# Seven block products for half the hidden channels of the expert layer's second product, and edge counts summed two tiles ahead of their mask

## What is computed

```python
_ACTS = [_gelu, jax.nn.silu, _mish, _gelu]
pooled = x.mean(axis=1)
logits = pooled @ router_w.T + router_b
top_v, top_i = jax.lax.top_k(logits, TOP_K)
...
h = jnp.einsum('bld,edh->belh', x, w1) + b1[None, :, None, :]
h = jnp.stack([_ACTS[i](h[:, i]) for i in range(e)], axis=1)
out = jnp.einsum('belh,ehd->beld', h, w2) + b2[None, :, None, :]
y = jnp.einsum('be,beld->bld', gate, out) + x
```

## Time and profile before

| | us |
|---|---|
| median of 3 runs | 2633.81 |
| lowest and highest | 2632.14, 2635.10 |
| profiled execution, its time | 2630.19 |
| profiled execution, its span | 2628.4 |

### The profile page before, as it was taken

The page is one execution under the profiler, slowest core; times in us unless marked ns, Lnnn a source line. Parts: engine busy times, 40 slices in busy tenths (PEclk is TensorE's granted clock), DMA queues, the critical chain, the costliest instruction groups (busy, mean ns, idle before and its releaser), DMA issues.

```text
span 2628.4 us, 26650 instructions
## 1 busy us (share of the span) xinstructions
PE 2555.2 (97%) x10594; PEld 1813.6 (69%) x10594; DVE 1587.2 (60%) x2708; ACT 769.6 (29%) x1291; POOL 347.7 (13%) x197
## 2 busy tenths in 40 slices
PE   7999999999999997999999999999999999999999
PEld 4667667558965996777777775565755786556676
DVE  4456471779948996987888998254342561341322
ACT  1043342006732863222222221430002331332000
POOL 0888888000000000000000000000000000000000
PEclk9999999999999998999999999999999999999999
DMA  9232313543020406000120003200450100213201
GB/s 257 26 44 14 50 2 50 143 145 123 20 80 20 116 1 215 1 0 1 72 102 0 24 24 115 70 1 1 115 164 18 37 1 1 63 37 126 87 24 59
DMA packets 139168, 160.74 MB, mean 61 GB/s; under 512 B 96618, under 2 KB 108484, under 8 KB 137516
## 3 DMA queue, kind: packets, MB, share of 16 engines
q1 hardware_dynamic: 68323, 158.60, 19.4%
q0 software_dynamic: 70720, 0.43, 2.8%
HBM read 122.75 MB, written 35.87 MB: 60 GB/s over the span
## 4 chain that ended last, share of the span: by engine, by line
PE 51%; DVE 7%; ACT 2%; issue 1%; DMA 0%; SPq 0%; DVEq 0%; ACTq 0%
PE psum L521 51%; DVE arena L1863 2%; DVE arena L1865 1%; DVE arena L1864 1%; PE psum L532 0%; DVE arena L1856 0%; ACT arena L1126 0%; ACT arena L1131 0%; ACT arena L1015 0%; DVE arena L1519 0%; DVE arena L1929 0%; DVE arena L1361 0%; DVE arena L1862 0%; DVE arena L1855 0%; DVE arena L1888 0%
## 5 line engine op out<-in xcount | busy, mean ns | idle before, releaser
L521 PE MATMUL psum<-arena 128*125 128x384 f32 (+12 forms) x9762 | 2454.4, 413 | 34.8 <-DMA arena<-in_ffn_w 7.1
L521 PEld LDWEIGHTS psum<-arena 128*125 128x125 f32 (+3 forms) x9762 | 1719.8, 188 | 745.5 <-issue 136.7
L2278 POOL DMA_INDIRECT count_matrix<-arena x170 | 343.0, 2018 | 121.1 <-DVE arena L1458 59.7
L1863 DVE RECIPROCAL arena<-arena 128x500 f32<-128x500 f32 x60 | 196.7, 3278 | 2.1
L1613 DVE CUSTOM_DVE_ANT_0 arena<-arena 125x1250 bf16<-125x1250 bf16 (+1 forms) x100 | 139.2, 1458 | 12.9 <-DMA arena<-source_rows 8.3
L2288 POOL MEMSET arena<- 125x60 f32 x1 | 0.2, 208 | 1039.4 <-PE psum L521 1039.4
L1697 DVE TENSOR_TENSOR arena<-arena 125x1250 f32<-125x1250 f32 x80 | 116.3, 1453 | 13.7 <-ACT arena L1108 13.6
L1105 ACT ACTIVATE arena<-arena 125x1250 f32<-125x1250 f32 x80 | 106.9, 1336 | 56.7 <-PE psum L521 56.5
L1700 DVE SCALAR_TENSOR_TENSOR arena<-arena 125x1250 f32<-125x1250 f32 x80 | 116.9, 1461 | 2.8
L1015 ACT ACTIVATE arena<-psum 128x250 f32<-128x250 f32 (+1 forms) x102 | 40.6, 494 | 231.4 <-PE psum L532 230.9
L1248 ACT ACTIVATE arena<-psum,arena 128x250 f32<-128x250 f32 x120 | 49.3, 465 | 198.6 <-PE psum L521 198.6
(11 more groups left out here) (226 smaller groups left out, 1435.0 us busy)
## 6 DMA issues: line engine op xcount, KB each, us to landing
arena<-in_ffn_w SPq DMA_DIRECT2D x3, 4608.0 KB, 14.9
residual<-arena SPq DMA_DIRECT2D x30, 336.0 KB
arena<-residual SPq DMA_DIRECT2D x30, 336.0 KB
arena<-target_rows SPq DMA_DIRECT2D x12, 610.4 KB
arena<-in_gat_w SPq DMA_DIRECT2D x3, 2304.0 KB, 10.5
arena<-residual SPq DMA_DIRECT2D x10, 672.0 KB
residual<-arena SPq DMA_DIRECT2D x10, 672.0 KB
count_matrix<-arena SPq DMA_DIRECT2D x2, 3125.0 KB, 26.9
```

Of the source, the lines that this page charges most:

```text
L521: return pe.matmul(o, lhsT, rhs, start=start, stop=stop, skip_group_check=share)
L1863: now(dve.reciprocal(t_, t_))
L2278: pool.indirect_dma_start(counts[k], bass.IndirectOffsetOnAxis(ap=IDX_I[0:T, c:c + 1].bitcast(U32), axis=0), COUNT_I[0:T, c:c + 1], None, ...
```

## The change

Of the 12 channel blocks of the second product, blocks 0 to 5 are taken as a 2 x 2 block matrix (two tiles by low and high three blocks) times another (low and high blocks by two output halves), and made with seven products of three matmuls instead of eight; blocks 6 to 11 are multiplied as before. The seven products need four sums of the weights (once per expert, `weight2_sums`) and four of the hidden values (once per unit, `sums_of_hidden`), made by VectorE. Bank `a` is read by VectorE between products: four times `add_part`, beside the four `add_bank` that drain the banks `d`, `b`, `c`, `a`. To make room the activation is rewritten: ScalarE takes the exponential straight from HB and squares it plus one constant, into a double buffer EB of one bank each; VectorE does min and add, reciprocal, multiply and add, multiply. The clamp and two instructions of `ratio` go. Gelu works in place.

In the attention part `count_sum` runs a block further ahead, and SP issues the loads of count block 5 and of the first source rows earlier. The loads of three rows and of one sixth of `mix1_wq` for the second level come later, since their places are in use.

```diff
-COUNTS_BESIDE = {0: (3,), 1: (4,), 2: (5, 6), 3: (7, 8), 4: (9,)}
+COUNTS_BESIDE = {0: (3,), 1: (4, 5), 2: (6,), 3: (7, 8), 4: (9,)}
...
+                product(1, bank_a, True).then_inc(down_filled, 1)
+                pe.wait_ge(hidden_sums, u + 1)
+                pe.wait_ge(w2_sums, u // 5 + 1)
+                product(5, bank_b, True).then_inc(down_filled, 1)
+                rest(1, 1, bank_d, True)
+                pe.wait_ge(down_read, n + 1)
+                product(6, bank_a).then_inc(down_filled, 1)
+                pe.wait_ge(down_read, n + 2)
+                product(3, bank_b, False, False)
+                rest(0, 1, bank_b)
+                pe.wait_ge(down_read, n + 3)
+                product(7, bank_a).then_inc(down_filled, 1)
+                product(2, bank_c, True, False)
+                rest(0, 0, bank_c)
+                pe.wait_ge(down_read, n + 4)
+                product(4, bank_a, False, False)
+                rest(1, 0, bank_a)
...
                 def expo(i):
-                    act.wait_ge(clamped, 6 * u + i + 1)
-                    act.activation(EB[:, 2 * i:2 * i + 2, :], TB[:, 2 * i:2 * i + 2, :], ACT.Exp).then_inc(expd, 1)
+                    n = 6 * u + i
+                    if n >= 2:
+                        act.wait_ge(exp_read, n - 1)
+                    act.wait_ge(a_drained, A_AT[("f1", u, i)] + 1)
+                    x = EB[n % 2]
+                    act.activation(x, HB[u % 2][:, 2 * i:2 * i + 2, :], ACT.Exp, scale=SCL[:, e:e + 1]).then_inc(act_step, 1)
+                    own[0] += 1
+                    act.wait_ge(act_step, own[0])
+                    act.activation(x, x, ACT.Square, bias=MISH[:, e:e + 1]).then_inc(expd, 1)
...
-                if j + 1 < NT:
-                    count_sum(j + 1)
+                if j + 2 < NT:
+                    count_sum(j + 2)
...
+                dve.tensor_scalar(t_, EB[n % 2], BIG, 1.0, ALU.min, ALU.add).then_inc(exp_read, 1)
+                dve.wait_ge(exp_read, n + 1)
+                now(dve.reciprocal(t_, t_))
+                now(dve.tensor_scalar(t_, t_, c(NCK), c(KO), ALU.mult, ALU.add))
+                ins = dve.tensor_tensor(t_, t_, h, ALU.mult)
...
                 if u < 10:
+                    for i in range(5):
+                        ratio(u, i)
+                        if u > 0 and u <= 5 and i == 2:
+                            add_bias(u - 1)
+                        if (u, i) in ((1, 3), (6, 3)):
+                            weight2_sums(u // 5)
+                if u > 0:
+                    down = {x: bank(("f2", u - 1, x)) for x in "dbca"}
+                    add_part(u - 1, 1, "a", 0, 0)
+                if u < 10:
+                    ratio(u, 5)
+                if u > 0:
+                    add_part(u - 1, 2, "b", 1, 1)
+                    dve.wait_ge(down_read, 4 * u - 2)
+                    add_bank(u - 1, "d", 1, 1)
+                    add_part(u - 1, 3, "a", 0, 1)
...
+                if u > 0:
+                    dve.wait_ge(down_read, 4 * u - 1)
+                    add_bank(u - 1, "b", 0, 1)
+                if u < 10:
+                    sums_of_hidden(u)
```

More of the change, by code:

```diff
@@ L295, in gps_kernel @@
         CO = small(16)
+        KO, MISH, CC, NCK, KG, SCL = (CO[:, 2 * i:2 * i + 2] for i in range(6))
         IS = small(2, 4)
@@ L779, in _, with down0, blocks, product @@
             mm(b[:, 0:4], ONES[:, 0:1].to_broadcast([128, 128]), POOLC[:, 0:4], True, True).then_inc(v_filled, 1)
+            def down0(u):
+                low, high = slice(0, 3), slice(3, 6)
+                tile = [slice(0, T), slice(T, 2 * T)]
+                h = HB[u % 2]
+                col = [slice(0, HALF), slice(HALF, D)]
+                def blocks(x):
+                    return [x[:, e] for e in range(3)]
+                s3 = [HS3[0][:, 0], HS3[1][:, 0], HS3[1][:, 1]]
+                left = [blocks(h[:, low, tile[0]]), blocks(h[:, high, tile[0]]), s3, blocks(h[:, high, tile[1]]),
+                        blocks(HS0), blocks(HS1), blocks(h[:, low, tile[1]])]
+                right = [W2[:, low, col[0]], W2[:, high, col[0]], W2[:, high, col[1]], W2T[2], W2T[0], W2T[1],
+                         W2[:, low, col[1]]]
+                bank_d, bank_b, bank_c, bank_a = (fill("V", ("f2", u, i)) for i in "dbca")
+                n = 4 * u
+                def product(i, b, begin=False, end=True):
+                    for e in range(3):
+                        last = mm(b[0:T, 0:HALF], left[i - 1][e], right[i - 1][:, e, :], begin and e == 0, end and e == 2,
+                                  share=True)
+                    return last
+                def rest(tt, half, b, begin=False):
+                    for m in range(6, HM):
+                        last = mm(b[0:T, 0:HALF], h[:, m, tile[tt]], W2[:, m, col[half]], begin and m == 6, m == HM - 1,
+                                  share=True)
+                    last.then_inc(v_filled, 1)
+                product(1, bank_a, True).then_inc(down_filled, 1)
[15 more added lines that the diff above has]
+                rest(1, 0, bank_a)
@@ L798, in _ @@
                     pe.wait_ge(act_made, u)
[L799 to L805, removed]
+                    down0(u - 1)
             def q1(c):
@@ L1231, in gelu @@
                 act.wait_ge(t_made, u + 1)
-                act.activation(EB, HB[u % 2], ACT.Gelu).then_inc(gelu_made, 1)
+                act.activation(HB[u % 2], HB[u % 2], ACT.Gelu).then_inc(gelu_made, 1)
             for u in range(10):
```

120 lines of the change are left out of this document (73 added, 47 removed).

## The result

| | before | after |
|---|---|---|
| median, us (4 runs each, same chip) | 2632.97 | 2695.22 |
| lowest and highest | 2629.64, 2635.10 | 2695.04, 2697.93 |
| span of the profiled execution | 2628.4 | 2693.3 |
| mean granted clock | 0.995 | 0.984 |

A forecast was written before the change was run, and what follows sets the result against it. PE's work was taken as the bound. Terms -19.4 (matmuls removed), +81, +12.5, -6.6 sum to +67.5 us: 2697.7 on the profiled 2630.2, 2701 for the median, 3.6 higher; own range 2684 to 2718, low end widened to 2676.

The forecast's parts named there:

- The reads: Expert layer: PE waits for DVE's reads of parts 1 and 2, queued behind activation pieces; delays sum to +81 us.
- The clock: Behind product 3's start the granted clock halves for some microseconds: 1.7 us in turns 2 to 5, 1.9 in 7 to 9; +12.5.
- the rival by which the clock doesn't fall: At the stops before product 3 the clock stays up, as after a 1.61 us stop: 2688 us, chance 0.12.
- The picture behind the term: Turns 2 to 5: slow product 6 shrinks the stop before product 3 to about 2 us, clock already low: 1.7 us each.
- The claim that turns 1 and 6 lose nothing behind product 3: In turns 1 and 6 the stop before product 3 is only 1.2 us, so the clock costs nothing there.
- the claim that a low clock ahead of a wait is covered: After stops before product 6 or 5, the clock loss falls in matmuls preceding the next wait and costs nothing.
- the rival with the clock low throughout: The clock stays low through the whole second product of nine units: about 2910 us, chance 0.02.
- The counts: Attention part: count sums made a block earlier and first source rows loaded earlier save 6.6 us; ends -6.6 and 0.
- the three terms: Attention part: -2.9 us waits for count sums, -2.0 stop at the attention's start, -1.7 clock behind that stop.
- the step on the first source rows: Source rows issued some 2.8 us earlier; DVE reaches the attention's start 5 to 6 us earlier, closing PE's 2.04 us stop.
- The moved load: Last sixth of `mix1_wq`, issued after the last unit's bank b: priced at nothing, up to 5 us if SP is held.
- "Faster": All reads in time, needing DVE pieces under 4.2 us in units 7 to 9, less before: 2608 us, chance 0.05.

The follow-up runs named there:

- the last kernel: The kernel without stops with one load, the last sixth of `mix1_wq`, issued earlier, ahead of residual tile 9: 2610.42 us, ratio 0.9923 to before.
- the filled kernel: The changed kernel plus 47 matmuls without use on TensorE, in the stops before products 6 and 3 of turns 2 to 5 and 7 to 9: 2684.17 us.
- the kernel without stops: The changed kernel with VectorE's reads, bias and weight sums in another order, TensorE's program the same: 2614.25 us, ratio 0.9944 to before.

## Why the prediction was right

It said 2701 us and slower; the median is 2695.22. Point by point:

**The reads.** Right in kind and place, and slightly too large. The undelayed period of a turn is 59.39 us (in the last kernel's trace the first banks of two units are drained at 1471.25 and 1530.64; before it was 61.3). With it each turn's delay, without the clock's part, is:

| turn | predicted, us | measured | from |
|---|---|---|---|
| 1 | 26.6 | 26.4 | 1108.68 - 1009.45 = 99.23, less 72.9 (1087.4 - 1014.54) |
| 2 to 5 | 7.1 each | 6.86 | 1174.93 - 1108.68 = 66.25 |
| 6 | 10.6 | 10.5 | 1448.43 - 1376.89 = 71.54, less 1.7 of clock |
| 7 to 9 | 5.2 each | 4.94 | 1512.76 - 1448.43 = 64.33 |
| sum | 81 | 79.1 | |

The piece is 4.93 us and not 5.07 (1231.70 to 1236.63): its first instruction takes 0.41 and not 0.47, and the next piece's begins 0.08 before the last one's recorded end. Six of them make 0.7 to 0.8 less. Small things go the other way: in turn 7 the first piece starts 3.63 us behind the second bank's drain (1481.83 - 1478.20), where 3.5 was taken, and PE goes on 0.67 us behind the start of the read, where 0.55 was taken. (The old piece comes to 7.1 us and not 7.0, the clamp being 0.42; no term hangs on it.)

**Waits and delay are not the same number.** The prediction expected near 70 us in PE's waits; it was 67.4, in 18 places. The rest of 79.1 lies where PE is recorded as busy: matmuls at the low clock that a later wait covers (1.4 and 1.6 us in product 6 of turns 2 and 3, 2.2 in the 12 matmuls behind the long stop of turn 6, 1.4 in those of turn 1) and some 0.26 for the restart at each of the 18 stops, 4.7; together 11.3 of the 11.7.

**The clock.** 12.5 us were taken, at two sizes. Against the 57.72 us of an undisturbed stretch (51.91 for the 210 records, 48.86 for the last one, by the filled kernel) the losses behind product 3 are 1.7, 0, 1.5 and 1.7 in turns 2 to 5, 1.7, 1.5 and 2.7 in turns 7 to 9: 10.8. The kernel that keeps PE busy gives 10.8 by its layer and 11 by the medians. So the term was right within 2 us, and the rival by which the clock doesn't fall (2688) is excluded. In one of the seven turns the clock didn't fall, and in the last it lost more than was taken. The picture behind the term (in turns 2 to 5 a slow product 6, then a stop of about 2 us, then the low clock) holds in turn 2 alone: in turn 3 the clock was back at 1.00 behind product 3's start, in turns 4 and 5 product 6 ran at full speed (2.20 us) and the stop was 3.38. That the sum comes out so close is in part luck. The claim that turns 1 and 6 lose nothing behind product 3 held: 57.72 both times. So did the claim that a low clock ahead of a wait is covered: the 5.58 us stay when the six records take 3.78.

On the rival with the clock low throughout: behind the starts of product 3 the clock is at the lower level for some microseconds only (0.67 over 5.24 us from 1512.76, 1.00 over the 6 us behind), and the loss is 10.8 us and not the 262 of that rival. The Trainium skill ("TensorE: Matmul & The Clock Gate", section "A second HAM failure mode: psum-queue depth-cycling") has the kernel lose throughput between bursts while its single matmuls are at the full clock. The trace agrees in that form. It doesn't agree that each of the two stops per turn costs, as the prediction read the rule: behind the stops ahead of product 6 the clock fell in two of seven turns (0.60 at 1169.35, 0.57 at 1237.30), and what that cost was covered by the next wait.

**The counts.** -6.6 was too much. The layer starts 5.1 us earlier; with the counts alone 4.55, and 2.4 by the medians. Of the three terms that of the clock came whole: behind the stop at the start of the attention it stayed at 1.00 (4.59 us from 608.91), and the 800 records there take 131.26 us for 132.95. The waits for count sums gave 2.5 for 2.9: none is left, but one of 0.46 us for the mask (L1654) is new. The stop itself went from 2.04 to 0.89 us and didn't close, 1.15 for 2.0. That is the step on the first source rows: DVE gains 3.3 to 3.7 us there, not 5 to 6, since it still stands 3 to 4 us for their DMA (539.07 and 538.64 for 542.33).

**The moved load.** Priced at nothing, and nothing in the changed kernel. But that held only while PE was held up: there SP issues the sixth 2.2 us ahead of the layer's end (1693.86 for 1696.01), in the kernel without stops 0.9 us behind it (1611.51 for 1610.63), and the same load costs 4.7 us. That PE's own stops had covered it is argued from these places. The upper end of 5 was the right bound for that case.

**Sum.** -19.4 + 79.1 + 10.8 = 70.5 in the layer, 70.1 by the trace; less 5.1 ahead of it, 65.4, and 64.9 by the spans. The forecast of 2701 lies 6 us high: 1.9 of delay and 1.7 of clock too much, 1.5 of counts the other way, 0.4 that the terms don't hold, and for the rest an offset of 3.6 us between median and profiled execution that didn't come again (2695.22 and 2695.04).

**What the prediction didn't see.** It treated DVE's place in the queue as given. It said that DVE was late by design and that this cost nothing before; it didn't ask what the same work would cost in another order. "Faster" was tied to pieces under 4.2 us. The runs show that the pieces may stay at 4.93: with the reads put between them (and the sums and the bias moved) the delay falls from 79 us to a few, and 15.3 of the 19.4 us arrive. The remaining 4.1 are a stop of 2.20 and one of 0.27, the low clock behind the first (0.59 in the 4.2 us from 1589.80, 1.7 us), and about 0.5 of restarts; these add up to 4.7, some half a microsecond more than is missing.

## What to carry to other kernels

When a matmul algorithm with fewer products makes TensorE wait for partial reads, the question is not how busy the reading engine is (57% here) but what stands in its queue ahead of each read. Write down, for every read that TensorE will wait for, the last step ahead of it and when that step can start; move the read in front of work with later deadlines. Then look one stage on: loads and other steps that were hidden by the old waits come due when these are gone.

## What the runs showed of the hardware

- A stop costs more than its idle time. Three matmuls of 384 columns take 2.20 us behind a stop at full clock, where 3 x 0.646 = 1.94: 0.26 us for each restart, 18 of them in the changed kernel. The prediction had no such term.
- The clock doesn't follow the length of the last stop alone. Behind 1.61 us it stayed at 1.00; behind 1.86, in the kernel with two reads moved, it did so in three turns and fell to 0.67 over 5.14 us in the fourth (1300.86); behind 3.38 it fell in all five cases of the changed kernel, but not in one of those of the kernel with the bias moved; behind 1.96 it was low (0.66) and behind 1.80 high (1.00), both after a stop of 2.96 and six slow records. In the run with the bias moved the pair 1.10 and 3.38 was followed by 0.50 over 5.36 us in one turn and by 0.67 in the next.
- Up to 2.6 us of matmuls without a use in each of 14 stops bought 11 us. They are no remedy where the order can be mended, but they price the clock cleanly.
